# Holding GpSimd's row fetches back until a count matrix is built

## The chip, the core and the metric

One NeuronCore of a Trainium2 chip runs the kernel. The metric is the device time of one execution in microseconds (us); the figure used is the median of several runs without a profile. A profile is a further execution, recorded instruction by instruction.

## The reference, cut to what matters

A graph of 3125 nodes (features of width 128) and 50000 edges, sorted by destination, passes through four layers: message passing with a mish activation and a two-layer perceptron, two SAGE convolutions, a graph convolution with batch normalisation, and graph attention with 8 heads. Each layer's output is added to its input and layer-normalised. Only the first layer's edges are touched here:

```python
def _L0_gnn_ref(nodes, edges, globals_g, W_e_k, W_e_b, eps, W1, b1, W2, b2, senders, receivers):
    sent = nodes[senders]                                 # one row of 128 floats for each edge
    e = mish(sent + edges @ W_e_k + W_e_b)
    agg = jax.ops.segment_sum(e, receivers, num_segments=n)
    h = (1.0 + eps) * nodes + agg
    ...
```

The layers in the middle need sums over the edges too. They use a matrix of edge counts (how many edges go from node a to node b), which the kernel builds once.

## The kernel before

The edges are padded to 392 tiles of 128, and four tiles make a **block**: 98 blocks (NF). The nodes are 25 tiles of 128 (NT). The stages run one after the other, each behind a barrier: `prepare`, `front` (which is `front_tables` and then `front_edges`), `layers`, `middle`, `edges_attention`, `tail_nodes`.

`front_tables` computes on VectorE and TensorE the keys, the order of the work and the words that steer it. Beside it GpSimd fetches the first seven blocks (SB = 7): `fetch` (line 374) issues four indirect DMAs for a block, one for each tile of 128 edges, and each of them gathers 128 rows of 512 bytes from `table0` into a slot of the ring `fr_ring`, which has 50 slots (RB).

`front_edges` has two phases, in this order on TensorE, ScalarE and VectorE:

- **The build.** 591 items (ITEMS). For each one VectorE makes a one-hot matrix of 128x400 (line 776, and for every eighth also line 780), TensorE multiplies it into a bank of PSUM (line 685), and for each pair of finished banks, 100 times, ScalarE moves the counts out (line 731) and clears the banks (line 734), which raises the semaphore `taken` by 2. `taken` starts at 8 and ends at 8 + BLOCKS = 208. VectorE's items after the first 16 run in a hardware loop, and then some are written out again.
- **The edges.** TensorE waits for `taken` at 208 (line 710). `pre(n)` adds a block's fetched rows and its edge product in a PSUM bank (lines 691, 694); ScalarE and VectorE apply mish (lines 741 to 753, 819, 824) and write the message over the fetched rows in the ring; `item(i)` sums a block's messages by node (line 707), and VectorE adds that to `acc` (line 837). There are 98 blocks and 122 items (FI = NF + NT - 1), since a block whose edges end in several node tiles is an item of each. TensorE runs pre 0 to 2, then item 0, pre 3, item 1, pre 4 and so on: 95 steps with an item and a pre, and then 27 items alone.

On GpSimd the fetches of blocks 7 to 97 stand in one loop with no tie to either phase. Block n waits until block n - 7 has landed, and from block 50 on also until the ring slot of block n - 50 is free: SyncE counts `released` up (line 655) when TensorE has finished the item after which that slot isn't needed. Each block of that loop thus issues four indirect DMAs. Behind the loop GpSimd has one more instruction in this stage, an addition to `x_now` (line 672), and then the barrier.

The names and numbers used further down: SB = 7 blocks fetched early, RB = 50 ring slots, so that blocks 7 to 49 (43 blocks, 172 DMAs) can be fetched before any slot is freed, and blocks 50 to 97 (48 blocks, 192 DMAs) can't.

Of the kernel before, what the change touches and what calls it, by code (L numbers as in the profile page):

```python
# [43 lines left out]
BLOCKS = NP // WB  # L44
# [110 lines left out]
def gnn_kernel(nc, xp, srccol, dstcol, dstflat, dsthead, lasthead, headtail, wcol, edgesT, wmat, wrow, wbc, gvec, out):  # L155
    ctx = ExitStack()
    with ctx:
# [212 lines left out]
        def fetch(pool, f, n):  # L370

            for t in range(TF):
                at = n * TF + t
                pool.indirect_dma_start(f.ring[:, n % RB, t, 0:D], None, tab[0][:, :],  # L374
                                        bass.IndirectOffsetOnAxis(ap=src_i[:, at:at + 1].bitcast(U32), axis=0)).then_inc(f.fetched_in[n % SB], 16)
# [216 lines left out]
        def front_edges(f):  # L592
            with ExitStack() as st:
# [3 lines left out]
                c = Counts(sem, "fe", "hot item moved taken pre least expd squared ln sig msg hot_n item_n add_n")  # L597
# [46 lines left out]
                with nc.Block() as block:  # L644
                    @block.sync
                    def _(sp):
                        sp.sem_inc(c["taken"], 8)
                        sp.wait_ge(ready, 4)

                        def wipe(n):  # L650
                            sp.dma_start(q_starts[n * BW:(n + 1) * BW, :].rearrange("(p t) f -> p (t f)", p=P), zero).then_inc(wiped, 16)

                        for n in range(RB, NF):
                            sp.wait_ge(c["item_n"], sp.value_load(f.free_at[0:1, n - RB:n - RB + 1], min_val=1, max_val=FI))
                            sp.sem_inc(released, 1)  # L655
                            wipe(n - RB)
                        for n in range(NF - RB, NB):
                            wipe(n)
                        for k in range(2):
                            sp.wait_ge(stored[k], (NT + 1 - k) // 2 * 16)  # L660
                        sp.wait_ge(wiped, NB * 16)

                    @block.gpsimd
                    def _(pool):
                        for n in range(SB, NF):
                            if n >= RB:
                                pool.wait_ge(released, n - RB + 1)
                            pool.wait_ge(f.fetched_in[n % SB], n // SB * 16 * TF)
                            pool.sem_inc(begun, 1)
                            fetch(pool, f, n)  # L670

                        pool.tensor_tensor(x_now[:, :, :], x_now[:, :, :], f.out_bias[:, :].unsqueeze(1).broadcast_to([P, NT, D]), ALU.add)
# [1572 lines left out]
```

## Time and profile before

| what | us |
|---|---|
| median of 3 runs | 1717.68 |
| lowest and highest run | 1715.59, 1720.96 |
| span of the profiled execution (no other time of it is given) | 2214.6 |
| `front_edges` in the profile: the build, 74.8 to 485.1 | 410 |
| `front_edges` in the profile: the edges, 489.1 to 941.2 | 452 |
| `edges_attention` in the profile: from its first to its last gather of rows | 656 |

A row of the timeline gives the start, the length, the engine, the line, the operation with what it writes and reads, and how often it stands there in a row; in brackets is the idle time of that engine before it and what ended it ("issue": nothing that the profile shows; "remote": an event from outside the recorded instructions). POOL is GpSimd, DVE is VectorE, ACT is ScalarE, PE is TensorE, SP is SyncE. A DMA that POOL issues is on record only for as long as POOL works at it.

### The profile page before, as it was taken

To read this page: it belongs to the slowest core of one execution; us is meant where nothing else is said; L and a number is where in the kernel's file an instruction comes from. 1 tells how busy PE (TensorE), PEld (TensorE's weight loads), DVE (VectorE), ACT (ScalarE), POOL (GpSimd) and SP (SyncE) were. 2 spreads that over 40 slices of the span, in tenths; PEclk is the share of its full clock that TensorE was granted. 3 is DMA by queue.
4 is the path that set the end of the run, shared out by engine and by line. 5 is a ranking of instruction groups with operands and counts; after the bars stand their busy time and mean duration, and the time that the engine had idled before them with its cause. 6 is when DMAs were issued, how large, how long until landed. Compare 5 with 4: busy or idle time off the path is not lost. (4 is left out here: it accounts for less than half of the span.)

```text
span 2214.6 us, 31367 instructions
## 1 busy us (share of the span) xinstructions
PE 1322.1 (60%) x7890; PEld 1079.8 (49%) x7890; DVE 1066.3 (48%) x2950; ACT 944.2 (43%) x2004; POOL 1037.5 (47%) x1171
## 2 busy tenths in 40 slices
PE   3222146666676689799989997314444454434666
PEld 2100013444554578688989895214433453424555
DVE  4411149873443467554964315314444454433666
ACT  0100137774454468275536645413333343333424
POOL 5677710005566640024458441665565666556234
PEclk9555569988888789999989998657676777667787
DMA  5221212224565563074545451546667666666521
GB/s 147 70 66 53 68 55 104 90 99 152 166 197 162 169 211 101 11 252 164 194 136 208 147 209 49 162 135 172 172 184 197 199 187 197 177 169 176 157 67 43
DMA packets 214072, 314.19 MB, mean 142 GB/s; under 512 B 31232, under 2 KB 159743, under 8 KB 213818
## 3 DMA queue, kind: packets, MB, share of 16 engines
q1 hardware_dynamic: 110724, 153.96, 21.9%
q0 software_dynamic: 33488, 81.02, 13.0%
q10 hardware_dynamic: 69734, 77.65, 10.9%
q8 instruction: 64, 1.05, 0.2%
q14 instruction: 62, 0.51, 0.1%
HBM read 223.87 MB, written 88.67 MB: 141 GB/s over the span
## 5 line engine op out<-in xcount | busy, mean ns | idle before, releaser
L374 POOL DMA_INDIRECT fr_ring<-table,src_i x392 | 376.2, 960 | 405.5 <-SPq L655 277.7
L1765 POOL DMA_INDIRECT e_kv<-kv_table,e_idx x392 | 387.1, 987 | 269.0 <-DVE e_msg L1848 153.7
L685 PE MATMUL fe_ps<-fe_space 128*128 128x400 bf16 x591 | 176.0, 422 | 244.5 <-issue 151.9
L685 PEld LDWEIGHTS fe_ps<-fe_space 128*128 128x128 bf16 x591 | 86.0, 145 | 334.3 <-issue 309.2
L776 DVE TENSOR_SCALAR fe_space<-fe_space,fr_key 128x400 bf16<-128x400 f16 x591 | 157.5, 323 | 176.1 <-remote 77.7
L1004 POOL CAST ly_af<-ly_au 128x640 fp32r<-128x640 uint16 x240 | 163.4, 729 | 126.4 <-DVE ly_part L1409 61.0
L1779 PE MATMUL e_q<-e_qs,e_mask 128*128 128x136 f32 x784 | 148.1, 360 | 80.9 <-issue 48.2
L1831 ACT ACTIVATE e_row<-e_p 128x864 f32<-128x864 f32 x56 | 49.6, 885 | 336.4 <-remote 292.5
L731 ACT ACTIVATE fe_space<-fe_ps 128x800 uint16<-128x800 f32 x100 | 83.6, 836 | 255.8 <-PE fe_ps L685 140.0
L707 PE MATMUL fe_ps<-fr_ring,fe_space 128*128 x976 | 147.9, 294 | 61.7 <-issue 32.3
L1779 PEld LDWEIGHTS e_q<-e_qs,e_mask 128*128 128x128 f32 x784 | 135.6, 258 | 87.9 <-issue 81.2
L1800 PE MATMUL e_p<-e_msg,e_mask 128*128 128x144 f32 x784 | 131.9, 330 | 73.1 <-ACT e_row L1832 42.2
L1793 PE MATMUL e_m<-ident,e_bs 56*128 56x56 f32 x56 | 16.4, 294 | 255.2 <-DVE e_bs L1866 157.5
L1863 DVE TENSOR_TENSOR_SCAN e_fs<-e_brk,e_a 56x128 f32<-56x128 f32 x56 | 23.0, 410 | 302.6 <-remote 209.7
L707 PEld LDWEIGHTS fe_ps<-fr_ring,fe_space 128*128 128x128 f32 x976 | 130.2, 205 | 71.8 <-issue 71.5
L1800 PEld LDWEIGHTS e_p<-e_msg,e_mask 128*128 128x128 f32 x784 | 122.5, 227 | 85.1 <-issue 78.7
L1070 PE MATMUL ly_ps<-ly_af,ly_x_high 128*128 128x256 f32 (+1 forms) x650 | 159.8, 288 | 2.4 <-POOL ly_af L1004 2.4
L1817 ACT ACTIVATE e_mask<-e_drow,e_neg_dst 128x128 f32<-128x128 uint16 x392 | 120.6, 388 | 85.7 <-issue 43.0
L1070 PE MATMUL ly_ps<-ly_af,ly_x_low 128*128 128x256 f32 (+1 forms) x650 | 156.2, 282 | 0.0
L694 PEld LDWEIGHTS fe_ps<-wm,fe_edge 128*128 128x128 f32 x784 | 117.4, 213 | 69.6 <-issue 69.2
L691 PE MATMUL fe_ps<-fr_ring,ident 128*128 128x512 f32 x196 | 117.8, 687 | 39.7 <-DVE fr_ring L824 20.5
L1793 PEld LDWEIGHTS e_m<-ident,e_bs 56*128 56x128 f32 x56 | 8.7, 156 | 265.3 <-issue 261.2
(397 smaller groups left out, 3177.2 us busy)
## 6 DMA issues: line engine op xcount, KB each, us to landing
ly_au<-edge_counts SPq DMA_DIRECT2D x88, 800.0 KB, 4.5
sums_att<-e_row ACTq DMA_DIRECT2D x56, 532.0 KB
q_starts<-fe_space SPq DMA_DIRECT2D x56, 476.0 KB
e_qs<-q_starts SPq DMA_DIRECT2D x56, 476.0 KB
fe_edge<-in_edgesT ACTq DMA_DIRECT2D x98, 256.0 KB
edge_counts<-fe_space ACTq DMA_DIRECT2D x25, 800.0 KB
e_drow<-dst_short SPq DMA_DIRECT2D x56, 224.0 KB
fr_ring<-table,src_i POOLq DMA_INDIRECT x392
```

The source lines that it names most:

```text
L374: pool.indirect_dma_start(f.ring[:, n % RB, t, 0:D], None, tab[0][:, :], bass.IndirectOffsetOnAxis(ap=src_i[:, at:at + 1].bitcast(U32), ax ...
L685: nc.tensor.matmul(ps[:, bass.ds(at, NW)], left(n), right(n % IS), start=False, stop=True, skip_group_check=True).then_inc(c["item"], 1)
L691: nc.tensor.matmul(bank_of(n), ident[:, :], ring[:, n % RB, :, 0:D], start=True, stop=True)
L694: last = nc.tensor.matmul(bank_of(n)[:, t * P:(t + 1) * P], edge[n % ER][:, t * P:(t + 1) * P], wm[:, W_E, :], start=False, stop=True, ski ...
L707: last = nc.tensor.matmul(sum_of(i), hot_n(i % NH)[:, t, :], flat[:, bass.ds(at + t * RW1, D + 1)], start=(t == 0), stop=(t == TF - 1))
L776: dve.tensor_scalar(right(s), numbers, f.key[:, bass.ds(n, 1)], None, ALU.is_equal).then_inc(c["hot"], 1)
L1004: part_in = pool.tensor_copy(counts_of(m)[:, a:a + NS, :], au[at_load(m) % AS][:, a:a + NS, :])
L1070: nc.tensor.matmul(ps_a[g % 2][:, 0:width(g)], piece[:, a, :], af[:, g % AF, 0:len(tiles(g)), a, :], start=(a == 0 and k == 0), stop=False)
L1765: pool.indirect_dma_start(kv[s][:, t, :], None, kv_table[:, :], bass.IndirectOffsetOnAxis(ap=idx[s][:, t:t + 1].bitcast(U32), axis=0)).the ...
L1779: last = nc.tensor.matmul(in_bank(ps_q, t, QW), mask[s][:, t, :], qs[s][:, t, :], start=True, stop=True)
L1800: last = nc.tensor.matmul(in_bank(ps_p, t, MW), mask[s][:, t, :], msg[s][:, t, :], start=True, stop=True)
L1817: last = nc.scalar.activation(mask[s][:, t, :], drow[s][:, t, :], ACT.Abs, bias=neg_dst[:, bass.ds(n * TB + t, 1)])
```

## The change

One wait is put in front of GpSimd's loop of fetches in `front_edges`. GpSimd waits until `taken` is 208, so until ScalarE has cleared the last banks of the build, and then issues blocks 7 to 97 as before. The seven blocks that `front_tables` fetches stay where they are. TensorE waits for the same value before its first `pre`.

```diff
                     @block.gpsimd
                     def _(pool):
+                        pool.wait_ge(c["taken"], 8 + BLOCKS)
                         for n in range(SB, NF):
                             if n >= RB:
                                 pool.wait_ge(released, n - RB + 1)
```

## Rows read from the trace of the kernel before

**Rows 1.** The page's head: the span, and the busy time of all engines.

```profile
span 2214.6 us, 31367 instructions
PE 1322.1 (60%) x7890; PEld 1079.8 (49%) x7890; DVE 1066.3 (48%) x2950; ACT 944.2 (43%) x2004; POOL 1037.5 (47%) x1171
```

**Rows 2.** Windows, line 776 alone: window, length, DVE busy (count), clock, DMA share, GB/s.

```profile
68.00:84.00 16.00, 7.69 (x27) 0.69 0.31 95
84.00:286.00 202.00, 25.38 (x74) 0.50 0.23 64
...
310.00:485.00 175.00, 121.43 (x481) 0.90 0.24 95
```

**Rows 3.** The same windows, line 374 alone: POOL busy (count) in the fourth column.

```profile
68.00:84.00 16.00, 12.65 (x12) 0.69 0.31 95
84.00:286.00 202.00, 153.23 (x161) 0.50 0.23 64
```

**Rows 4.** Timeline of all engines in the build, with POOL issuing, 200 to 205.

```profile
200.68 0.33 DVE L776 TENSOR_SCALAR fe_space<-fe_space,fr_key 128x400 bf16<-128x400 f16 x1 [2.43 <-remote]
...
202.22 0.95 POOL L374 DMA_INDIRECT fr_ring<-table,src_i  x1 [0.30 <-issue]
...
203.47 0.32 DVE L776 TENSOR_SCALAR fe_space<-fe_space,fr_key 128x400 bf16<-128x400 f16 x1 [2.47 <-issue]
...
204.09 0.53 PE L685 MATMUL fe_ps<-fe_space 128*128 128x400 bf16 x1 [5.11 <-issue]
```

**Rows 5.** Timeline of the build's first items, POOL issuing beside them, 76 to 80.

```profile
76.69 2.24 DVE L776 TENSOR_SCALAR fe_space<-fe_space,fr_key 128x400 bf16<-128x400 f16 x8
...
79.14 1.21 POOL L374 DMA_INDIRECT fr_ring<-table,src_i  x1 [0.30 <-issue]
79.44 2.24 DVE L776 TENSOR_SCALAR fe_space<-fe_space,fr_key 128x400 bf16<-128x400 f16 x8
```

**Rows 6.** The two lines of indirect DMAs: shortest/median/longest ns, first and last start.

```profile
L374 POOL DMA_INDIRECT fr_ring<-table,src_i x392: 943/947/1584, 20.3 to 801.0; - x196
...
L1765 POOL DMA_INDIRECT e_kv<-kv_table,e_idx x392: 950/957/1880, 1419.5 to 2074.2; - x196
```

**Rows 7.** Timeline of PE at both ends of the edges' phase.

```profile
489.08 2.07 PE L691 MATMUL fe_ps<-fr_ring,ident 128*128 128x512 f32 x2 [3.96 <-ACT fe_ps L734]
...
499.59 1.15 PE L707 MATMUL fe_ps<-fr_ring,fe_space 128*128 x8 [2.36 <-DVE fr_ring L824]
...
891.15 1.02 PE L691 MATMUL fe_ps<-fr_ring,ident 128*128 128x512 f32 x2
...
893.80 1.02 PE L691 MATMUL fe_ps<-fr_ring,ident 128*128 128x512 f32 x2
...
895.55 1.95 PE L707 MATMUL fe_ps<-fr_ring,fe_space 128*128 x16
```

**Rows 8.** Timeline of POOL: the end of its first run, its restart, its last instruction.

```profile
285.07 0.95 POOL L374 DMA_INDIRECT fr_ring<-table,src_i  x1 [0.30 <-issue]
503.84 0.95 POOL L374 DMA_INDIRECT fr_ring<-table,src_i  x1 [217.83 <-SPq L655]
...
801.95 6.97 POOL L672 TENSOR_TENSOR x_now<-x_now,fr_out_bias 128x3200 f32<-128x3200 f32 x1
```

**Rows 9.** Windows, all engines: PE, PEld, DVE, ACT, POOL busy (count), clock, DMA share, GB/s.

```profile
489.00:895.00 406.00, 310.20 (x1736) 241.76 (x1737) 204.79 (x387) 227.23 (x387) 188.95 (x193) 0.86 0.52 163
895.00:941.00 46.00, 31.36 (x223) 26.51 (x221) 24.41 (x56) 4.83 (x9) 0.00 (x0) 1.00 0.01 1
1419.00:2075.00 656.00, 267.09 (x1494) 241.72 (x1495) 257.74 (x706) 225.62 (x567) 387.04 (x393) 0.68 0.64 180
```

**Rows 10.** DMA issues: an indirect gather whose landing is on record, us to landing.

```profile
n_g<-sums_att,end_row POOLq DMA_INDIRECT x25, 3.1
```

**Rows 11.** Timeline of DVE in `edges_attention`, one instruction for each group of 7 tiles.

```profile
1693.59 1.07 DVE L1884 TENSOR_REDUCE e_red<-e_prod 128x56 f32<-128x896 f32 x1
...
1700.06 1.07 DVE L1884 TENSOR_REDUCE e_red<-e_prod 128x56 f32<-128x896 f32 x1
```

## The prediction

> **What bounds the kernel now.** I began with the page's head against the runs: the profiled execution spans 2214.6 us [rows 1], the median of the runs is 1717.7 us. The profile is 496.9 us too long, and the whole argument hangs on where that excess sits. So I looked for stretches in which the recorded machine does less than its own rows say it can.
>
> The windows of line 776, the one-hot matrices of the build, show the first [rows 2]. From 310 to 485, with GpSimd silent, VectorE makes 481 in 175 us, 0.364 us each. From 84 to 286 it makes 74 in 202 us, 2.73 us each, and in that time GpSimd issues 161 fetches [rows 3]. This looks like plain contention, and a reader would move the fetches away from the build for it. Two things disturb the picture. In the stalled stretch every engine is idle at once, VectorE for 2.4 us with no instruction that releases it and TensorE for 5.1 us with nothing that the profile shows, while GpSimd keeps its step of 1.25 us [rows 4]. And in the first 16 us the build runs at full rate beside the same fetches: 27 matrices beside 12 fetches [rows 2, 3], eight items in 2.75 us (76.69 to 79.44), which is 0.344 us each [rows 5]. A lock or a shared port would bite from the first fetch on.
>
> The same pattern stands in the two other places with indirect DMAs, and only there. I priced the excess of each by its own unstalled rows.
> - Build. 84 to 310 holds 591 - 27 - 481 = 83 items (74 of them before 286), which at 0.364 us are 30 us; 226 - 30 = 196 us excess.
> - Edges. The way to the first item takes 10.5 us (489.08 to 499.59), an unstalled step with item and pre takes 2.65 us (891.15 to 893.80), and there are 95: 252 us; the 27 lone items take 46 us, 895 to 941 [rows 7, 9]. Together 309 us, against 452 us: 143 us excess.
> - Attention. 392 gathers in 656 us [rows 6, 9]. Its groups of seven can follow each other in 6.5 us (1693.59 to 1700.06) [rows 11], so GpSimd's 7 x 1.255 = 8.8 us a group would bound it: 392 x 1.255 = 492 us, so 164 us excess.
>
> The sum is 503 us, against the 497 us by which the profile is longer than the runs. My reading: the stalls are part of the profiled execution, and an unprofiled run has none of them. The Trainium skill (NOTIFIC — the notification-queue block, 7.1 Overflow) says that the block which writes trace records can hold back the engines that produce them; that would fit engines idle all at once, but no row here shows such a record queue, and no term needs it.
>
> In a run without a profile the build then takes 591 x 0.364 = 215 us and the edges 309 us, both as if GpSimd weren't there. GpSimd fetches blocks 7 to 49 in 172 x 1.255 = 216 us beside the build and is done about when it is; in the profile it even waits 217.8 us for the first free slot [rows 8].
>
> **The change, part by part.** *The new wait* costs GpSimd one instruction. Behind it are queued all 364 fetches of blocks 7 to 97 and the addition to `x_now`. The first to want them is TensorE's pre 7, and pre 97 is the last. The seven early blocks cover 3 + 4 steps, some 20 us.
>
> *What the build gains.* It loses the 172 fetches beside it. By the stalled rows that is 196 us. By the first 16 us it is nothing, since the items there were no slower (0.344 against 0.364 us) [rows 5, 2]; VectorE's eight matrices took 2.24 us, 0.28 each, and if a bound by VectorE made its 7.69/27 against 121.43/481 us (0.285 against 0.252) count for all 591, 20 us. I take 0, by the stretch that is nearest to an unprofiled run, with 20 us as the end on the gain's side.
>
> *What the edges lose.* GpSimd has 364 fetches to issue from the moment at which TensorE starts its first pre; both wait for the same value. Its step is 202/161 = 1.255 us [rows 3]: 0.947 us of instruction [rows 6] and 0.30 us between two [rows 4]. 364 x 1.255 = 457 us. Before, only 192 stood here, 241 us from the first freed slot on, 14.8 us into the phase (489.08 to 503.84) [rows 7, 8]; they ended at about 256 us, and pre 97 comes at 10.5 + 94 x 2.65 = 260 us, so they just stayed hidden. Now the last fetch ends at 457 us, while TensorE could run that pre at 260. The ring is no limit any more: slot 50 is asked for after 172 x 1.255 = 216 us, when its block is long done, so SyncE's `released` and its own stores are off the path.
>
> *The end of the phase.* After the last fetch comes its landing, 3.1 us by the only gather with a landing on record, of another shape [rows 10]; then pre 97, 2 us, and the 27 lone items, 46 us [rows 9]: TensorE keeps its order, so they can't be moved ahead. The phase is 457 + 3 + 2 + 46 = 508 us, against 309: 199 us more. The addition to `x_now`, 6.97 us [rows 8], falls into those 46 us, as before into TensorE's last 140; without that cover it would cost 7 us.
>
> *The one unknown of size* is the step of a fetch without a profile. If the 0.30 us between two were the recorder's, it would be 0.95 us: 346 us, a phase of 397 us, +88 us, 1806 us. Then attention would fall to 372 us, or to the 0.64 x 656 = 420 us that its DMA engines are busy [rows 9]; its excess would be 236 us and the three together 575 us, 78 us more than there are. With 1.255 us the sum misses by 6. I take 1.255 and keep 0.95 for the range. *The clock*: the lone items ran at granted clock 1.00, and the edges at 0.86 [rows 9]. TensorE will now be about half idle before them; in the stalled build it stood at 0.50 [rows 2]. If all 27 items ran at half, their 31 us of matmul would double, +31 us. The nearest rows for TensorE so idle are attention's, 0.68 at 267 of 656 us busy: 31/0.68 - 31 = +15 us. I take 0, since the lone items keep TensorE busy two thirds of the time and stood at 1.00, and keep +15 for the range.
>
> **The sum.** Build 0, edges +199: 1717.7 + 199 = 1917 us, or 11.6% more. Against the profile's own span the same sum doesn't hold, see below.
>
> **Rivals.**
> 1. *The stalls are real.* Then the build gains 196 us, and the edges pay for 91 blocks instead of 48 at the stalled pace, which for those 48 was (801.95 - 503.84)/48 = 6.2 us a block [rows 8]. 91 x 6.2 = 564, with the 51 us behind it 615, against 452: +163 - 196 = -33 us, 1685 us. By excess per fetch (143/192 = 0.74 us at best, 196/172 = 1.14 us at worst) it is -70 to +76. The price decides for faster as long as a stalled block costs under 6.5 us. For it: rows 2 and 4 as they stand. Against it: the full rate beside GpSimd at the start [rows 5], and that 503 us of stalls are as long as the 497 us which the runs don't have. The Trainium skill (SBUF — State Buffer, on the trap of VectorE blocking GpSimd's DMAs) has such a mechanism: VectorE's fast modes lock GpSimd out of a shared port and the fetches starve. By that rule the move helps the fetches; here GpSimd is the one that keeps its step, so the trace doesn't agree.
> 2. *Only the build's stall is real.* -196 + 199 = +3 us, 1721 us. Against it: the same pattern in all three places.
> 3. *A fetch is so cheap that it hides.* 364 fetches are hidden if their step is under 0.71 us, (309 - 51)/364; then 1718 us. Against it: instruction rows never under 0.943 us [rows 6].
> 4. *It doesn't do what it says*: the semaphore passes 208 early. It starts at 8 and gains 2 at each of 100 clears, so it can't.
>
> **How the numbers follow.** Forecast 0.80, with steps from 0.95 to 1.26 us in it; rival 1 0.11; rival 2 0.04; rival 3 0.04; rival 4 0.01. A difference under 0.3% (5 us) can't be told from none. Faster: most of rival 1, and a little of rival 2: 0.09. Same: rivals 3 and 4 and a part of 2: 0.07. Slower: 0.84. The range goes from the lower end of the step (1806), a little below for some gain in the build, to the sum with the clock's 15 us and as much again for what starts late: 1795 to 1945. It leaves the rivals out, 0.2.
>
> **What the new profile would show.** Right: the build's matrices at 0.36 us throughout, some 215 us instead of 410, with no stalled stretch; GpSimd silent until about 290 and then 364 fetches in an unbroken row; no wait for SyncE's line 655; TensorE's pre waiting for fetches, not for ScalarE or VectorE. The profiled span itself will mislead: since it still stalls where GpSimd issues, I expect it 70 us shorter to 76 us longer, about 2180 us, while the runs get 199 us longer. **Wrong** would be runs near 1685 (the stalls are real), near 1720 (rivals 2, 3), or near 1825 (the right mechanism with a step of 1.0 us). An edges' phase with TensorE waiting for ScalarE would refute the fetch bound.

## The result: 10.7% slower, and the profile after

The changed kernel takes 1901.4 us, median of 4 runs (1896.1 to 1905.8), against 1719.3 us for the kernel before: ratio 1.107, 95% interval 1.104 to 1.110. Forecast were 1917 us, in a range of 1795 to 1945.

The profile of the kernel before that stands ahead of the prediction was taken of a disturbed execution (2214.6 us, where this kernel's runs take 1710 to 1722, but for three of 46 that took 1766, 1958 and 2355 us and are left out of the ratios), so the kernel before is read here in a second profile of the same file. That one spans 1712.5 us. The profile of the changed kernel spans 1897.7 us; the two differ by 185.2 us, the medians by 182. From here on the profiled execution is one of the runs, and not a further one: the changed kernel's is its run of 1899.5 us, the other three took 1896.1 to 1905.8.

First the page's head and the 40 slices of the changed kernel, which answer to [rows 1]. A slice is 47 us.

```profile
span 1897.7 us, 31367 instructions
PE 1325.5 (70%) x7890; PEld 1112.8 (59%) x7890; DVE 1061.2 (56%) x2950; ACT 951.2 (50%) x2004; POOL 1041.0 (55%) x1171
...
PE   3477668767776777799998999645566556655576
...
POOL 4100007777777776124547634167777777777454
PEclk9988989888888888999989999877877877888886
```

GpSimd (POOL) is silent for slices 3 to 6, the build, and then runs without a gap to slice 16. The same lines of the kernel before, second profile (a slice is 43 us):

```profile
span 1712.5 us, 31367 instructions
...
PE   3476766899999788999899977265665565656485
...
POOL 4777775777776023445773504777777777777353
```

Here GpSimd runs beside the build too, and TensorE (PE) is at 9 through most of the edges, slices 9 to 13, where after the change it is at 6 to 8 for ten slices.

The edges' phase in the changed kernel, timeline of GpSimd's restart, last fetch and last instruction, then TensorE at both ends. They answer to [rows 8] and [rows 7].

```profile
284.87 0.95 POOL L374 DMA_INDIRECT fr_ring<-table,src_i  x1 [228.90 <-ACT fe_ps L735]
...
739.81 0.95 POOL L374 DMA_INDIRECT fr_ring<-table,src_i  x1 [0.30 <-issue]
740.79 7.00 POOL L673 TENSOR_TENSOR x_now<-x_now,fr_out_bias 128x3200 f32<-128x3200 f32 x1
```

```profile
284.10 2.08 PE L692 MATMUL fe_ps<-fr_ring,ident 128*128 128x512 f32 x2 [4.30 <-ACT fe_ps L735]
...
738.34 1.69 PE L692 MATMUL fe_ps<-fr_ring,ident 128*128 128x512 f32 x2 [2.53 <-DMA fr_ring<-table,src_i]
...
743.35 1.12 PE L692 MATMUL fe_ps<-fr_ring,ident 128*128 128x512 f32 x2 [0.45 <-DMA fr_ring<-table,src_i]
...
746.45 1.15 PE L708 MATMUL fe_ps<-fr_ring,fe_space 128*128 x8 [0.19 <-issue]
```

364 fetches start within 454.9 us, 1.253 us apart. The last has landed at 743.4, some 2.6 us after its instruction ends, TensorE goes on at once with `pre` 97, and the 27 lone items follow. `acc` gets its last addition at 791.3 to 791.6. So the phase takes 507.5 us, from `pre` 0 at 284.1. Who waits for the fetches, in the list of waits (engine, line, releaser, us in total, times, longest):

```profile
POOL fr_ring L374 <- ACT fe_ps L735: 228.9, 1, 228.9
PEld fe_ps L692 <- DMA fr_ring<-table,src_i: 131.2, 55, 6.7
PE fe_ps L692 <- DMA fr_ring<-table,src_i: 120.4, 50, 6.5
```

GpSimd's wait for the ring (SyncE's line 655) is gone, as forecast; TensorE waits for gathers in its stead.

### The profile page after: what moved, and what is told of

Its sections match the earlier page's. It is cut to its first block and busy times, and to the rows that moved or that the text cites. A ratio compares the mean times of both kernels' runs of the same rounds, so it can differ in the third digit from the quotient of the medians.

```text
span 1897.7 us, 31367 instructions
## 1 busy us (share of the span) xinstructions
PE 1325.5 (70%) x7890; PEld 1112.8 (59%) x7890; DVE 1061.2 (56%) x2950; ACT 951.2 (50%) x2004; POOL 1041.0 (55%) x1171
## 5 line engine op out<-in xcount | busy, mean ns | idle before, releaser
L1780 PE MATMUL e_q<-e_qs,e_mask 128*128 128x136 f32 x784 | 161.0, 382 | 222.0 <-DVE e_wq L1883 197.9
L1780 PEld LDWEIGHTS e_q<-e_qs,e_mask 128*128 128x128 f32 x784 | 147.4, 278 | 228.4 <-issue 185.1
L692 PE MATMUL fe_ps<-fr_ring,ident 128*128 128x512 f32 x196 | 126.7, 733 | 124.9 <-DMA fr_ring<-table,src_i 120.4
L686 PE MATMUL fe_ps<-fe_space 128*128 128x400 bf16 x591 | 149.1, 398 | 76.0 <-DVE fe_space L777 60.4
L820 DVE TENSOR_SCALAR fe_space<-fe_ps 128x512 f32<-128x512 f32 x98 | 67.8, 692 | 237.8 <-PE fe_ps L695 237.7
L742 ACT ACTIVATE fe_space<-fe_space 128x512 f32<-128x512 f32 x98 | 61.7, 630 | 231.6 <-DVE fe_space L820 231.6
L695 PEld LDWEIGHTS fe_ps<-wm,fe_edge 128*128 128x128 f32 x784 | 129.7, 235 | 59.4 <-issue 59.4
L1880 DVE TENSOR_TENSOR e_prod<-e_q,e_kv 128x768 f32<-128x768 f32 x56 | 53.6, 957 | 172.0 <-DMA e_kv<-kv_table,e_idx 170.3
L1801 PEld LDWEIGHTS e_p<-e_msg,e_mask 128*128 128x128 f32 x784 | 123.1, 228 | 16.5 <-DVE e_msg L1849 12.2
L695 PE MATMUL fe_ps<-wm,fe_edge 128*128 128x128 f32 x784 | 129.9, 321 | 0.0
L1071 PEld LDWEIGHTS ly_ps<-ly_af,ly_x_high 128*128 128x128 f32 x650 | 124.5, 192 | 3.3 <-POOL ly_af L1005 2.6
```

The costliest lines, as they stand in the source:

```text
L686: nc.tensor.matmul(ps[:, bass.ds(at, NW)], left(n), right(n % IS), start=False, stop=True, skip_group_check=True).then_inc(c["item"], 1)
L692: nc.tensor.matmul(bank_of(n), ident[:, :], ring[:, n % RB, :, 0:D], start=True, stop=True)
L695: last = nc.tensor.matmul(bank_of(n)[:, t * P:(t + 1) * P], edge[n % ER][:, t * P:(t + 1) * P], wm[:, W_E, :], start=False, stop=True, ski ...
L1071: nc.tensor.matmul(ps_a[g % 2][:, 0:width(g)], piece[:, a, :], af[:, g % AF, 0:len(tiles(g)), a, :], start=(a == 0 and k == 0), stop=False)
L1780: last = nc.tensor.matmul(in_bank(ps_q, t, QW), mask[s][:, t, :], qs[s][:, t, :], start=True, stop=True)
L1801: last = nc.tensor.matmul(in_bank(ps_p, t, MW), mask[s][:, t, :], msg[s][:, t, :], start=True, stop=True)
```

## The experiments

Each edit is given against the changed kernel, unless said otherwise. Ratios are against the kernel before on the same chip, 1715 us there.

### before_again: the kernel before, profiled once more

> The kernel before, unchanged, profiled a second time. The changed kernel's profile spans 1897.7 us and is as long as its runs, with no stalled stretch, though my prediction expected the stalls to come back wherever GpSimd issues. Theory S (the stalls belonged to that one recorded execution): a second profile spans about 1718 us, the build takes 215 us and the edges 309 us with GpSimd fetching beside both, attention some 510 us as in the changed kernel's profile. Theory R (the stalls belong to the fetches beside the build, through the recorder or not): the span is near 2214 us again, with the build at 410 us and the edges at 452 us.

Measured: span 1712.5 us, ratio of its runs 1.0003 (0.9987 to 1.0019). Windows of the build (67 to 282), the edges with pre (286 to 560), the lone items and attention; columns as in [rows 9]:

```profile
67.00:282.00 215.00, 148.42 (x591) 85.89 (x591) 202.50 (x664) 163.09 (x195) 165.63 (x163) 0.93 0.42 142
286.00:560.00 274.00, 262.74 (x1735) 211.94 (x1736) 205.54 (x387) 229.60 (x386) 191.34 (x196) 0.99 0.75 242
561.00:606.00 45.00, 30.47 (x215) 25.62 (x213) 24.02 (x55) 3.94 (x7) 0.00 (x0) 1.00 0.00 1
1083.00:1597.00 514.00, 303.83 (x1636) 283.86 (x1636) 282.10 (x766) 247.41 (x608) 394.52 (x393) 0.77 0.85 237
```

and the same stretches of the changed kernel, where the edges with pre have two rows:

```profile
67.00:280.00 213.00, 149.13 (x591) 86.16 (x591) 191.28 (x661) 163.22 (x196) 0.00 (x0) 0.93 0.23 93
284.00:500.00 216.00, 159.14 (x866) 125.17 (x866) 102.97 (x193) 114.52 (x193) 163.01 (x172) 0.88 0.63 198
500.00:739.00 239.00, 167.00 (x848) 130.78 (x849) 100.35 (x191) 113.57 (x192) 180.76 (x192) 0.84 0.47 144
746.00:792.00 46.00, 30.27 (x211) 25.23 (x209) 23.94 (x55) 3.62 (x6) 1.79 (x1) 1.00 0.01 1
1270.00:1783.00 513.00, 294.27 (x1631) 273.08 (x1632) 281.50 (x766) 246.20 (x606) 393.28 (x393) 0.79 0.85 238
```

What follows: theory S, though the edges take 320 us and not the 309 of the forecast. The build takes 215 us with 163 fetches beside it, and 213 us with none. TensorE is busy for 262.7 of 274 us in the edges with pre before, and for 326 of 455 us after, where the same matmuls take longer at a granted clock of 0.88 and 0.84 instead of 0.99. Attention is the same. With the first profile the stalled stretches are gone too: 541 matrices of line 776 stand in the 202 us from 84 to 286 in which [rows 2] have 74.

### half_build, wait_60, wait_20: the wait passes earlier

The edit of half_build; the other two wait for 8 + 60 and 8 + 20.

```diff
-                        pool.wait_ge(c["taken"], 8 + BLOCKS)
+                        pool.wait_ge(c["taken"], 8 + BLOCKS // 2)
```

> The changed kernel with its wait passing at taken = 108 instead of 208, so at half of the count matrix. Fetch theory: GpSimd starts about 108 us earlier, some 86 of its 364 fetches lie beside the build and cost it nothing, the edges take 508 - 108 = 400 us, the run 1901 - 108 = 1793 us. Rival (a fetch beside the build stalls it by 1.14 us, the excess of the first profile): the build gets 98 us longer and the run stays within 10 us of 1891.

> The wait passes at taken = 68, after 30 of the 100 clears, about 134 us into the profile. By the same sum the edges end at 134 + 508 = 642 instead of 606: 36 us longer, 2.1%, 1752 us. If every us of delay were paid for, 73 us longer, 1790 us; if only the time after the build counted, no change.

> The wait passes at taken = 28, after 10 of the 100 clears, some 92 us into the profile, instead of 284. In an undisturbed profile of the kernel before, GpSimd starts at 60.6, the edges end at 606 us, and GpSimd's last fetch is some 15 us earlier than TensorE needs it; in the changed kernel the edges end 508 us after GpSimd's start. Fetch theory: the edges end at the later of 606 and start + 508, so any start up to 98 us is free: 92 + 508 = 600, no change, within 0.3% of the kernel before. Rival (every us of GpSimd's idle time is paid for, since it is never idle in the kernel before): 32 us longer, 1.9%.

Measured: half_build 1800.8 us, 1.049 (1.046 to 1.052); wait_60 1754.6 us, 1.025 (1.022 to 1.028); wait_20 1720.2 us, 1.0036 (1.0021 to 1.0050). GpSimd's first fetch after the wait, in the timelines of half_build, wait_60 and wait_20:

```profile
177.28 1.24 POOL L374 DMA_INDIRECT fr_ring<-table,src_i  x1 [121.28 <-ACT fe_ps L735]
```

```profile
133.89 1.00 POOL L374 DMA_INDIRECT fr_ring<-table,src_i  x1 [77.50 <-ACT fe_ps L735]
```

```profile
91.63 1.01 POOL L374 DMA_INDIRECT fr_ring<-table,src_i  x1 [35.30 <-ACT fe_ps L735]
```

| kernel | first fetch of the loop | last addition to `acc` ends | between |
|---|---|---|---|
| before_again | 60.6 | 606.3 | 546 |
| wait_20 | 91.6 | 606.5 | 515 |
| wait_60 | 133.9 | 648.3 | 514 |
| half_build | 177.3 | 690.7 | 513 |
| changed kernel | 284.9 | 791.6 | 507 |

So the edges end some 507 to 515 us after GpSimd starts, or at 606 us, whichever is later. A delay of 31 us moves the end of the edges by 0.2 us: TensorE's own work covers it. Of the 31 us, 15 are slack at the end (the last fetch starts at 554.5 instead of 539.5, and `pre` 97 still at 558), and 11 come from GpSimd's waits for a free ring slot, SyncE's line 655, which are 12.2 us in before_again and 0.9 in wait_20. Beyond that each us of delay costs about one. In wait_20 the cover is used up: TensorE waits once for a gather, 1.0 us, and it is that of the last block:

```profile
558.12 1.13 PE L692 MATMUL fe_ps<-fr_ring,ident 128*128 128x512 f32 x2 [1.03 <-DMA fr_ring<-table,src_i]
```

Its runs are 5 us above the kernel before, 0.36% where I had said within 0.3%. The profiles, 3.8 us apart, have 3.4 of it in attention (514.7 us from its first to its last gather, against 512.8) and behind it, in code that the wait doesn't touch; why isn't shown. Wait_60 and half_build end their edges 6 us later than forecast (648.3 against 642, 690.7 against 685), since the distance is 513 to 514 us there and not 508.

### split22: 22 blocks ahead of the wait

```diff
-                        pool.wait_ge(c["taken"], 8 + BLOCKS)
                         for n in range(SB, NF):
+                            if n == SB + 22:
+                                pool.wait_ge(c["taken"], 8 + BLOCKS)
```

> The same wait as in the change (taken = 208), but blocks 7 to 28 (22 of 91, 88 of 364 fetches) are issued ahead of it, right at the start of the build. It tells the number of fetches left after the build from the time at which the first starts. Fetch theory: 276 x 1.2525 = 346 us of issuing after 284, with 51 us behind it the edges end at 681 instead of 606, 75 us longer, about 1791 us. Rival (the late restart matters and not the number): about 1890 to 1901 us, as with all 364 behind the wait.

Measured: 1795.3 us, 1.046 (1.044 to 1.048). GpSimd's restart in its timeline:

```profile
286.29 0.95 POOL L374 DMA_INDIRECT fr_ring<-table,src_i  x1 [107.09 <-ACT fe_ps L736]
```

The edges end at 682.6 us, as 276 fetches and the 51 us behind them say (forecast 681). Half_build starts once, in the middle of the build, and has 81 fetches beside it; split22 starts at once, has 88 beside it, and then stands still for 107 us. Their edges end 8 us apart (690.7 and 682.6), as seven fetches of 1.25 us say, and their runs are within 6 us of each other. It is the number of fetches left after the build that counts, not the restart.

### two_of_four: half of the gathers left out

```diff
-            for t in range(TF):
+            for t in range(TF if n < SB else 2):
...
+                        pool.memset(ring[:, SB:RB, 2:TF, 0:D], 1.0).then_inc(filled, 1)
                         pool.wait_ge(c["taken"], 8 + BLOCKS)
```

with the counts of the waits on the gathers set to match, and TensorE waiting for `filled`.

> The changed kernel, but from block 7 on only two of a block's four gathers are issued; the other two tiles of the ring keep what they held, so the sums of the first layer leave half of the source rows out. Fetch theory: 182 x 1.255 = 228 us of issuing is less than the 260 us at which TensorE wants the last block, the edges take 309 us and the run 1901 - 199 = 1702 us. Rival (the edges are slower for another reason than the number of fetches, as the latency of a block or the late start alone): the run stays above 1850 us.

Measured: 1721.5 us, 1.0038 (1.0018 to 1.0059). The memset which I put in so that TensorE reads defined numbers holds the build back (see the last section): `pre` 0 starts at 292.9 instead of 284.1. From there the edges take 321 us, and in before_again 320. The run is 20 us above the 1702 of the forecast: some 9 are the memset's, and some 12 come from the 309 us that I had for edges bound by TensorE. So with the same wait and the same late start, half of the fetches gives the whole loss back. The rival, that the late start by itself costs, is out.

### half_rows: all gathers, with half of the rows

```diff
-                pool.indirect_dma_start(f.ring[:, n % RB, t, 0:D], None, tab[0][:, :],
+                pool.indirect_dma_start(f.ring[0:(P if n < SB else 64), n % RB, t, 0:D], None, tab[0][:, :],
...
+                        pool.memset(ring[64:P, SB:RB, :, 0:D], 1.0).then_inc(filled, 1)
```

with the index cut in the same way.

> The changed kernel, all 364 gathers after the wait, but each for 64 rows instead of 128; the other half of the ring keeps what it held, so half of the source rows are left out. If a fetch's 1.25 us on GpSimd are a price per instruction, the run stays at 1901 us. If the 0.95 us within it go by the rows, the step falls to 0.77 us, the edges to 364 x 0.77 + 51 = 331 us and the run to 1725 us. Bytes in flight fall by half in both cases.

Measured: 1904.0 us, 1.109 (1.106 to 1.112). Line 374, with the columns of [rows 6]:

```profile
L374 POOL DMA_INDIRECT fr_ring<-table,src_i x392: 893/900/1320, 19.8 to 740.0; - x196
```

A gather of 64 rows takes 0.900 us where one of 128 takes 0.947, and the step is 1.205 instead of 1.253 us. The edges take 489 us (301.8 to 791.0), 18 us less than the 507.5; the memset's delay of 17.7 us hides that in the run's time. So the step is, but for 4%, a price per instruction: that is all that half the rows and half the bytes take off. The 1725 us of the rival are out.

## Why the prediction was right, point by point

**Where the excess of the profile sits.** I read the stalls as no part of an undisturbed run, and that held. What I gave as their reason, that a profiled execution has them and others don't, is refuted: the second profile of the same kernel has none, and neither it nor the later ones are longer than the other runs of their kernels. What disturbs an execution isn't settled by these runs. The agreement of 503 with 497 us was partly luck. Against the second profile the build had 196 us too much (410 against 215), as I priced it; the edges 132 us, not 143; attention 142, not 164, since it takes 514 us and not 492; and `front_tables` and `tail_nodes`, where I had looked for nothing, 7 and 24 us.

**The build gains nothing.** Right: 2 us. Pre 0 starts at 284.1 instead of 286.4. Line 776 (777 in the changed kernel) in one window of 202 us, first with the fetches beside it, in before_again:

```profile
84.00:286.00 202.00, 148.56 (x541) 0.92 0.43 144
```

and without, in the changed kernel:

```profile
84.00:286.00 202.00, 136.51 (x536) 0.91 0.24 98
```

A matrix takes 0.275 us beside a fetch and 0.255 us without. That is the 20 us of VectorE's time which I had as the bound, 12 us here, and most of it is hidden: in the build VectorE is busy for 191.3 instead of 202.5 us, and the build is 2 us shorter. VectorE waits for TensorE instead, 15.6 us against 8.5. TensorE waits some 60 us for VectorE's matrices in both kernels, and 15 to 18 us for ScalarE's cleared banks, so no one engine alone sets the length of the build, and which of these waits took up the gain isn't shown.

**The step of a fetch.** 1.253 us measured, 1.255 taken. Keeping 0.30 us between two instructions in the price was right: without them the same sum gives 1806 us, and the runs took 1901. Beside the build a fetch is dearer: 149 in the 196 us from 84 to 280 of before_again, 1.315 us each. So the change saves GpSimd some 0.06 us for each of 172 fetches, 11 us at most, which fits the distance in the table that falls from 515 to 507.

**The phase after.** 507.5 us measured, 508 forecast, with its parts: 457 of issuing (455.9), 3.1 of landing (2.6), 48 of pre 97 and the lone items (48.2); the other 0.8 us is GpSimd's restart after TensorE's. The clock of the lone items is 1.00, so the 15 us that I kept for it weren't needed; in this phase it fell to 0.84 to 0.88 only where TensorE waits for fetches anyway. The addition to `x_now` falls into the lone items, as said.

**The phase before, the term that was mis-sized.** I had 309 us from the unstalled rows and it is 320: 199 us of loss became 187. Each step after the first was priced at the best step, 2.65 us. Line 691 alone in windows of 40 us, before_again, shows where steps are slower; two matmuls are a block:

```profile
300.00:340.00 40.00, 12.28 (x24) 1.00 0.78 253
340.00:380.00 40.00, 15.35 (x30) 1.00 0.90 294
...
460.00:500.00 40.00, 14.32 (x28) 1.00 0.79 270
```

15 blocks in 40 us is the full pace. The first window has 12, and the one from 460 has 14. The timeline of TensorE gives the first loss its cause and its size, and the list of waits of the phase (286 to 560) has the same wait:

```profile
301.91 1.15 PE L707 MATMUL fe_ps<-fr_ring,fe_space 128*128 x8 [1.57 <-DVE fr_ring L824]
302.90 1.02 PE L691 MATMUL fe_ps<-fr_ring,ident 128*128 128x512 f32 x2
...
306.38 1.15 PE L707 MATMUL fe_ps<-fr_ring,fe_space 128*128 x8 [1.56 <-DVE fr_ring L824]
307.37 1.02 PE L691 MATMUL fe_ps<-fr_ring,ident 128*128 128x512 f32 x2
```

```profile
PE fe_ps L707 <- DVE fr_ring L824: 8.6, 5, 2.4
PEld fe_ps L694 <- DMA fe_edge<-in_edgesT: 3.4, 6, 1.2
```

The first item waits 2.4 us for its message from VectorE, which is in the 10.5 us that I had for the way to it. The next four wait 1.56 to 1.57 us each, and their steps take 5.7 us once and 4.47 three times instead of 2.65: 8.5 us lost before 317, the first of them in part by a granted clock of 0.83 (297 to 305; 1.00 from then on). A further 4.5 us go in eight longer steps, six of them between 463 and 485, near which TensorE's weight loads wait for edge features from DRAM, 3.4 us in the whole phase. Against these 13 us the lone items end some 2 us sooner than priced, which leaves the 11. So the mis-sized term is the step at the start of the phase, where the messages aren't ready in time; why they are from 318 on isn't shown. 187 less the 2 us of the build are the 185 us of the two profiles.

**Hidden so far, but barely.** I said that the 192 late fetches just stayed hidden, by 4 us. They are hidden by 16 us (the last instruction ends at 540.5, 2.6 us of landing as in the changed kernel, and pre 97 starts at 558.9), since the phase is longer. Wait_20 shows the cover from the other side.

**The profiled span.** Wrong. I expected it to stay near 2180 us and to mislead. It followed the runs.

**Rivals.** Rival 1, real stalls, would have given 1685 us, and rival 2 1721 us; both fall with before_again. Rival 3, a cheap fetch, falls with the step, and rival 4 with GpSimd's first fetch at 284.9, 0.8 us after TensorE's first pre.

No version here beats the kernel before. In the edges it is bound by TensorE, 39.8 to 40.0 of 40 us busy in its full windows, and moving fetches can't help that.

## What to carry to other kernels

Before moving one engine's instructions away from a crowded stretch, add up how long that engine needs for all of them at its own step, and compare with the time at which the last is wanted; an engine that issues 364 instructions at 1.25 us needs at least 456 us wherever they stand, and the stretch in which it could run ahead of the engine that wants them was its cover. If a profile is much longer than the runs, price its stretches from their undisturbed rows and see whether the excess adds up to the difference, and then still take a second profile: the reason for the excess can't be read from the first. A phase priced by its best step comes out short; count the items in equal windows, see which windows miss that step, and read there what is waited for.

## What the runs showed of the hardware

A memset by GpSimd held up a VectorE instruction until it had ended. It was in two_of_four and half_rows, at the start of `front_edges`, and wasn't meant as an experiment. VectorE's cast of 128x1024 takes 0.63 us in before_again:

```profile
60.73 0.63 DVE L765 CAST fe_space<-iota 128x1024 f16<-128x1024 f32 x1
```

In half_rows it takes 18.11 us, until 0.55 us after GpSimd is through, and the build starts 17.4 us late:

```profile
59.27 18.44 POOL L666 MEMSET fr_ring<- 64x22016 f32 x1 [3.30 <-POOLq L186]
59.50 0.72 DVE L768 MEMSET fr_ring<- 128x800 f32 x1 [3.16 <-PEq L186]
60.15 18.11 DVE L769 CAST fe_space<-iota 128x1024 f16<-128x1024 f32 x1
```

VectorE's own memset before it, at 59.50, takes 0.72 us as in before_again, beside the same GpSimd instruction: not every VectorE instruction is held. In two_of_four, with a memset of half the length on all partitions:

```profile
59.34 9.27 POOL L666 MEMSET fr_ring<- 128x11008 f32 x1 [3.29 <-POOLq L186]
```

```profile
60.22 8.94 DVE L769 CAST fe_space<-iota 128x1024 f16<-128x1024 f32 x1
```

The Trainium skill (SBUF — State Buffer, Who interferes with whom) says that the engine which starts first has the shared port for its whole instruction and the other is blocked; both traces agree, with 18.11 and 8.94 us against 0.63. An indirect DMA does nothing of the kind to VectorE: beside fetches its matrices took 0.275 instead of 0.255 us, and the fetches 1.315 instead of 1.253 us.
